# The even chunk's h stays in PSUM, small copies move to ScalarE, and batch 0's routed pairs are done as seven products

## What is computed

```python
def L0(x, y, weight, mask, bias):
    w_bot = einsum('bg,got->bot', y, weight * mask[None])
    return einsum('bnt,bot->bno', x, w_bot) + bias

def L1(x, router_logits, skill_gate, skill_up, skill_down, shared_gate, shared_up, shared_down):
    rw = softmax(router_logits); w, sel = top_k(rw, 2); w = w / w.sum(-1)
    dense_w = zeros((B, E)).at[arange(B)[:, None], sel].add(w)
    mlp = lambda x, g, u, d: einsum('bsi,ih->bsh', gelu(einsum('bsh,hi->bsi', x, g)) * einsum('bsh,hi->bsi', x, u), d)
    out = sum over e of dense_w[:, e] * mlp(x, skill_gate[e], skill_up[e], skill_down[e])
    return out + mlp(x, shared_gate, shared_up, shared_down)

x = x + L0(x, cond_8, weight, mask, bias)
x = x + L1(x, cond_8, skill_..., shared_...)
```

## Time and profile before

| | |
|---|---|
| median of 3 runs | 427.54 us (426.96 to 427.88) |
| the profiled execution | 427.97 us, its span 426.0 us |
| granted clock of PE | 0.999 over the span |
| PE busy | 414.5 us |
| DVE busy | 318.6 us |
| POOL busy | 273.3 us |
| ACT busy | 223.9 us |
| DMA | 36.24 MB, mean 85 GB/s |

### The profile page before, as it was taken

The page is one execution under the profiler, slowest core; times in us unless marked ns, Lnnn a source line. Parts: engine busy times, 40 slices in busy tenths (PEclk is TensorE's granted clock), DMA queues, the critical chain, the costliest instruction groups (busy, mean ns, idle before and its releaser), DMA issues.

```text
span 426.0 us, 6965 instructions
## 1 busy us (share of the span) xinstructions
PE 414.5 (97%) x2133; PEld 349.1 (82%) x2133; DVE 318.6 (75%) x459; ACT 223.9 (53%) x407; POOL 273.3 (64%) x271
## 2 busy tenths in 40 slices
PE   8999999999999999999999899999999999999997
PEld 6688888888888887788888688788888788888886
DVE  3566543334369998887888999988787888888885
ACT  5665555444434366654554347646555445557441
POOL 1565364487603579999626748999771866998820
PEclk9999999999999999999999999999999999999999
DMA  7763243234201513223100252222200041232001
GB/s 254 225 191 138 58 125 99 74 101 123 75 0 51 174 40 118 91 75 102 25 26 0 76 170 74 74 74 83 89 25 25 0 149 49 76 106 69 25 26 49
DMA packets 20187, 36.24 MB, mean 85 GB/s; under 512 B 2242, under 2 KB 3010, under 8 KB 20162
## 3 DMA queue, kind: packets, MB, share of 16 engines
q1 hardware_dynamic: 19872, 35.66, 27.3%
q10 hardware_dynamic: 290, 0.26, 0.2%
HBM read 33.82 MB, written 2.10 MB: 84 GB/s over the span
## 4 chain that ended last, share of the span: by engine, by line
PE 66%; DVE 18%; issue 9%; ACT 4%; DMA 1%; SPq 1%; DVEq 0%; ACTq 0%
PE o_ps L556 7%; PE g_ps L503 7%; PE g_ps L502 7%; PE g_ps L506 7%; PE u_ps L506 7%; PE u_ps L502 7%; PE u_ps L503 7%; PE o_ps L563 7%; PE p_ps L563 5%; DVE h_lo L1027 4%; ACT h_hi L764 3%; DVE h_lo L1037 2%; PE l_ps L461 2%; DVE l_ps L955 2%; DMA l_raw<-l_w 1%
## 5 line engine op out<-in xcount | busy, mean ns | idle before, releaser
L1200 POOL TENSOR_TENSOR eg_lo<-raw_g,eg_hi 128x512 fp32r<-128x512 f32 x64 | 89.2, 1408 | 43.9 <-ACT eg_hi L711 43.9
L740 ACT ACTIVATE gelu<-g_ps 128x512 f32<-128x512 f32 x96 | 57.4, 598 | 47.2 <-PE g_ps L506 46.8
L759 ACT CAST h_hi<-u_ps 128x512 fp32r<-128x512 f32 x34 | 20.0, 588 | 79.2 <-DVE u_ps L986 44.9
L986 DVE SCALAR_TENSOR_TENSOR u_ps<-gelu,route_cur,u_ps 128x512 f32<-128x512 f32 x42 | 31.5, 749 | 34.6 <-PE u_ps L506 32.8
L1037 DVE TENSOR_TENSOR h_lo<-t_raw,h_hi 128x1024 fp32r<-128x1024 f32 x34 | 51.8, 1525 | 6.5 <-ACT h_hi L764 6.4
L764 ACT CAST h_hi<-t_raw 128x1024 fp32r<-128x1024 f32 x34 | 35.7, 1051 | 32.8 <-DVE t_raw L1023 32.8
L1239 POOL TENSOR_TENSOR ed_lo<-raw_d,ed_hi 128x384 fp32r<-128x384 f32 x22 | 36.8, 1671 | 22.1 <-ACT ed_hi L720 22.1
L503 PE MATMUL g_ps<-x_hi,eg_lo 128*128 128x512 f32 (+1 forms) x128 | 50.4, 394 | 0.0
L502 PE MATMUL g_ps<-x_hi,eg_hi 128*128 128x512 f32 (+1 forms) x128 | 50.1, 391 | 0.0
L502 PE MATMUL u_ps<-x_hi,eg_hi 128*128 128x512 f32 (+1 forms) x128 | 49.8, 389 | 0.0
L503 PE MATMUL u_ps<-x_hi,eg_lo 128*128 128x512 f32 (+1 forms) x128 | 49.8, 389 | 0.0
(11 more groups left out here) (234 smaller groups left out, 1130.0 us busy)
## 6 DMA issues: line engine op xcount, KB each, us to landing
raw_g<-experts SPq DMA_DIRECT2D x64, 256.0 KB, 2.7
raw_d<-experts SPq DMA_DIRECT2D x32, 256.0 KB, 2.8
l_raw<-l_w SPq DMA_DIRECT2D x8, 256.0 KB, 5.7
x_in<-xT SPq DMA_DIRECT2D x8, 256.0 KB, 4.3
raw_g<-shared SPq DMA_DIRECT2D x8, 256.0 KB, 4.4
raw_d<-shared SPq DMA_DIRECT2D x8, 256.0 KB, 2.9
outT<-out_sb SPq DMA_DIRECT2D x6, 256.0 KB, 3.0
mask<-l_mask SPq DMA_DIRECT2D x2, 128.5 KB, 6.2
```

What stands on the lines that cost most here:

```text
L740: act.activation(gelu[:, s % 2], g_ps[:], ACT.Gelu_apprx_tanh).then_inc(gelu_done, 1)
L1200: pool.tensor_tensor(eg_lo[:, j % RING], raw_g[:, j % RAW_G], eg_hi[:, j % RING].bitcast(F32), ALU.subtract).then_inc(gu_lo_done, 1)
```

## The change

In fast pairs the even chunk's h is formed in place in `u_ps[:, 0]`; `h_a` goes. Its first half is read from PSUM by ACT (high part) and DVE (T1, low part); its second half is copied by ACT into the small SBUF tile `b12`, which T1 and T3 read. PE's wait ahead of the up projection into `u_ps[:, 0]` becomes one for the low part of h. ACT's order in a fast step becomes gelu, split_t, split of h, b12, then the weights; gate and up weights are split two by two in odd steps, on ACT and POOL. `pick_cond` and `pick_route` go from DVE to ACT. In batch 0, pairs 4 to 11 (the routed ones) become fast: POOL gets `expert_s` and the split of the S parts for them, its gate and up splits from step 8 on go two by two into odd steps, and ScalarE, DVE and POOL drain its sums as those of the other batches are. P5 moves from the PSUM bank of P4 to that of P1; P1 and P5 are copied out in one instruction. The sums of a batch on POOL are seven instructions in place of five. In the last batch DVE's adds are arranged anew. Semaphore counts follow.

```diff
         def fast(b, p):
 
-            return not at_first(b) and not (at_last(b) and p >= LAST_FAST)
+            return not (at_first(b) and p < PAIRS) and not (at_last(b) and p >= LAST_FAST)
+
+        def first_fast(b, p):
+            return at_first(b) and p == PAIRS
...
-                if s < 2 and not at_first(b):
-                    was_fast = not (isinstance(b, int) and b == 1)
-                else:
-                    was_fast = fast(b, s // 2 - 1)
-                if was_fast and s % 2 == 0:
-                    pe.wait_ge(h_done, n - 1)
-                elif was_fast:
+                was_fast = not at_first(b) if s < 2 else fast(b, s // 2 - 1)
+                if was_fast and s % 2:
                     pe.wait_ge(t_done, 4 * pair_count(b, s // 2 - 1) + 4)
...
             def products_123(b, p):
                 wait_d(b, p)
                 pe.wait_ge(h_lo_done, STEPS * b + 2 * p + 2)
-                if p == 0:
+                if first_fast(b, p):
                     pe.wait_ge(x1_done, HH)
-                    pe.wait_ge(out_done, 1)
-                    pe.wait_ge(evac_done, 4 * b)
-                first, last = p == 0, p == (LAST_FAST - 1 if at_last(b) else NP - 1)
+                elif p == 0:
+                    pe.wait_ge(evac_done, 3 * b - 1)
+                last = p == (LAST_FAST - 1 if at_last(b) else NP - 1)
                 wt = d_weights(p)
-                product(P1, wt, None, A11, B11, first, last)
-                product(P2, wt, None, A12, B21, first, False)
-                product(P3, wt, None, S4, B22, False, last).then_inc(down_done, 1)
+                product(P1, wt, A11, B11, p == 0 or first_fast(b, p), False)
+                product(P2, wt, A12, B21, p == 0, False)
+                product(P3, wt, S4, B22, False, last).then_inc(down_done, 1)
 
             def products_4567(b, p):
                 pe.wait_ge(t_lo_done, pair_count(b, p) + 1)
                 if p == 0:
-                    pe.wait_ge(out_done, HH)
-                    pe.wait_ge(evac_done, 4 * b + 2)
-                    if not (isinstance(b, int) and b == 1):
-                        pe.wait_ge(x1_p4_done, b - 1)
-                first, last = p == 0, p == (LAST_FAST - 1 if at_last(b) else NP - 1)
+                    pe.wait_ge(evac_done, 3 * b)
+                    pe.wait_ge(x1_p4_done, b)
+                last = p == (LAST_FAST - 1 if at_last(b) else NP - 1)
                 wt = d_weights(p)
-                product(P6, wt, None, S2, T2, first, False)
-                product(P7, wt, None, S3, T3, False, last)
-                product(P4, wt, None, A22, T4, first, False)
-                product(P5, wt, None, S1, T1, False, last).then_inc(down_done, 1)
+                product(P5, wt, S1, T1, False, last)
+                product(P6, wt, S2, T2, p == 0 or first_fast(b, p), False)
+                product(P7, wt, S3, T3, False, last)
+                product(P4, wt, A22, T4, p == 0, last).then_inc(down_done, 1)
...
-                act.copy(h_hi[:, 0:TH], h_a[:, 0:TH]).then_inc(h_hi_done, 1)
+                act.copy(h_hi[:, 0:TH], u_ps[:, 0, 0:TH]).then_inc(h_hi_done, 1)
+                if not first_fast(b, p):
+                    act.wait_ge(t_done, 4 * pair_count(b, p))
+                act.copy(b12[:], u_ps[:, 0, TH:T]).then_inc(b12_done, 1)
...
-            def evacuate_123(b):
+            def evacuate_23(b):
 
                 act.wait_ge(down_done, STEPS * b + STEPS - 1)
-                act.copy(stage_1, P1).then_inc(evac_done, 1)
+                act.wait_ge(d_lo_done, d_index(b + 1, 0))
                 act.copy(stage_23, o_ps[:, 0]).then_inc(evac_done, 1)
 
-            def evacuate_4567(b):
+            def evacuate_1567(b):
                 act.wait_ge(down_done, STEPS * b + STEPS)
+                act.copy(stage_15, p_ps[:, 0]).then_inc(evac_done, 1)
                 act.copy(stage_67, p_ps[:, 1]).then_inc(evac_done, 1)
-                act.copy(stage_5, P5).then_inc(evac_done, 1)
...
-                    if SPLIT_LEAD <= s < SPLIT_LEAD + ECH:
+                    if SPLIT_LEAD <= s < CHUNKS:
+                        split_gu(0, s - SPLIT_LEAD)
+                    if CHUNKS <= s < SPLIT_LEAD + ECH and s % 2:
+                        split_gu(0, s - SPLIT_LEAD - 1)
                         split_gu(0, s - SPLIT_LEAD)
...
-                    if s < 2 + ECH:
+                    if s % 2 and s < 2 + ECH:
+                        split_gu(b, s - 3)
                         split_gu(b, s - 2)
 
+            def pick_cond(b):
+                act.copy(cond_cur[:], cond_all[:].rearrange("p b e -> p (b e)")[:, bass.ds(b * G, G)]).then_inc(cond_picked, 1)
+
+            def pick_route(b):
+                if at_first(b):
+                    act.wait_ge(weighed, 8)
+                else:
+                    act.wait_ge(h_done, STEPS * b)
+                act.copy(route_cur[:], route_w[:, bass.ds(b * TOP_K, TOP_K)]).then_inc(route_picked, 1)
+
...
-                weights_beside(b, s)
                 if not fast(b, s // 2):
+                    weights_beside(b, s)
                     split_h(b, s)
                 elif s % 2 == 0:
                     split_b11(b, s // 2)
+                    weights_beside(b, s)
                 else:
                     split_b2(b, s // 2)
+                    weights_beside(b, s)
+                if s == CHUNKS - 1:
+                    pick_route(b)
                 if with_next:
                     next_beside(b, s)
 
...
             def form_t1(b, p):
-                if not (isinstance(b, int) and b == 1 and p == 0):
+                if not first_fast(b, p):
                     dve.wait_ge(t_lo_done, pair_count(b, p))
-                dve.wait_ge(h_done, STEPS * b + 2 * p + 1)
-                dve.tensor_tensor(t_part(T1), h_a[:, TH:T], h_a[:, 0:TH], ALU.subtract).then_inc(t_done, 1)
+                dve.wait_ge(b12_done, pair_count(b, p) + 1)
+                dve.tensor_tensor(t_part(T1), b12[:], u_ps[:, 0, 0:TH], ALU.subtract).then_inc(t_done, 1)
 
             def form_t234(b, p):
-                dve.tensor_tensor(t_part(T3), u_ps[:, 1, TH:T], h_a[:, TH:T], ALU.subtract).then_inc(t_done, 1)
+                dve.tensor_tensor(t_part(T3), u_ps[:, 1, TH:T], b12[:], ALU.subtract).then_inc(t_done, 1)
                 dve.wait_ge(t_done, 4 * pair_count(b, p) + 1)
...
-                dve.tensor_tensor(h_lo[:, 0:TH], h_a[:, 0:TH], h_hi[:, 0:TH].bitcast(F32), ALU.subtract).then_inc(h_lo_done, 1)
+                dve.tensor_tensor(h_lo[:, 0:TH], u_ps[:, 0, 0:TH], h_hi[:, 0:TH].bitcast(F32), ALU.subtract).then_inc(h_lo_done, 1)
...
-            def store_ready_0(oh):
-                dve.wait_ge(x1_done, HH)
-                if oh == 0:
-                    dve.wait_ge(sum0_done, 1)
-                else:
-                    dve.wait_ge(down_done, STEPS)
-                dve.tensor_tensor(out_sb[:, oh], x1_at(x1, 0, oh), o_ps[:, oh], ALU.add).then_inc(out_done, 1)
...
+                at, n = (b % 2) * (HH * T) + T, T if at_first(b) else TH
+                dve.wait_ge(down_done, STEPS * b + STEPS)
+                dve.tensor_tensor(x1[:, bass.ds(at, n)], x1[:, bass.ds(at, n)], o_ps[:, 1, 0:n], ALU.add).then_inc(x1_p4_done, 1)
...
+            def add_products_23():
 
                 b = B - 1
                 dve.wait_ge(stored, 16 * HH * b + 1)
                 dve.wait_ge(x1_done, HH * B)
                 dve.wait_ge(down_done, STEPS * b + 2 * LAST_FAST - 1)
-                dve.tensor_tensor(out_flat, x1_all(b).rearrange("p (q c) -> p q c", c=TH), P1.unsqueeze(1).to_broadcast([P, 4, TH]), ALU.add).then_inc(rest_done, 1)
-                dve.wait_ge(rest_done, 1)
-                dve.tensor_tensor(out_sb[:, 0], out_sb[:, 0], o_ps[:, 0], ALU.add).then_inc(rest_done, 1)
-
-            def add_products_6():
+                dve.tensor_tensor(out_sb[:, 0], x1_at(x1, b, 0), o_ps[:, 0], ALU.add).then_inc(rest_done, 1)
+
+            def add_products_46():
                 dve.wait_ge(down_done, STEPS * (B - 1) + 2 * LAST_FAST)
+                dve.tensor_tensor(out_sb[:, 1, 0:TH], x1_at(x1, B - 1, 1)[:, 0:TH], P4, ALU.add).then_inc(rest_done, 1)
+                dve.tensor_tensor(out_sb[:, 1, TH:T], x1_at(x1, B - 1, 1)[:, TH:T], P6, ALU.add).then_inc(rest_done, 1)
                 dve.wait_ge(rest_done, 2)
-                dve.tensor_tensor(out_flat[:, 1:4], out_flat[:, 1:4], P6.unsqueeze(1).to_broadcast([P, 3, TH]), ALU.add).then_inc(rest_done, 1)
-
-            def add_products_457():
-                dve.wait_ge(rest_done, 3)
+                dve.tensor_tensor(out_flat[:, 1:3], out_flat[:, 1:3], P6.unsqueeze(1).to_broadcast([P, 2, TH]), ALU.add).then_inc(rest_done, 1)
+
+            def add_products_157():
+                dve.wait_ge(rest_done, 4)
                 dve.tensor_tensor(out_flat[:, 2:4], out_flat[:, 2:4], P7.unsqueeze(1).to_broadcast([P, 2, TH]), ALU.add).then_inc(rest_done, 1)
-                dve.wait_ge(rest_done, 4)
```

(40 more changed lines are left out.)

122 lines of the change are left out of this document (42 added, 80 removed).

## The result

The changed kernel takes 429.63 us (median of 6 runs, 429.5 to 429.98) where the kernel before took 427.62 us beside it (6 runs, 426.96 to 428.27): a ratio of 1.0049, 95% interval 1.0037 to 1.0062. It is slower by 2.0 us; 422.2 was predicted, and the range ended at 427.5. The profiled execution has a span of 427.5 us, 1.5 more than before.

The account below looks back on a forecast made before the run. PE was taken as the bound, busy 414.5 of 426.0 us, losing 11.0 us to late DVE work. Terms -10.3 - 1.3 + 6.3 = -5.3 us off the 427.54 median gave 422.2 us, range 417.5 to 427.5.

Parts of the forecast that it names:

- h in PSUM: T1 and h's low part on DVE take 415 ns each with one PSUM input; 10.3 us gained, ends 7 and 11.
- the 11.0 us: PE's time lost in batches 1 to 3 against undisturbed pairs of 8.00 us: 3.05 + 5.35 + 2.56.
- both covers: T1's wait for b12 hidden behind DVE's 1024-wide split; the even chunk's PSUM bank freed with 1.6 us or more to spare.
- rival (d): Even chunk's bank or b12 not covered, no gain from PSUM in batches 1 to 3: 432.5 us, chance 0.02.
- Weights behind h: ScalarE's new order, two by two: POOL starts later, but the chain closes under 8.0 us per pair; nothing charged.
- rival (c): The DVE, ScalarE, POOL ring becomes the period, 8.5 us in all 30 routed pairs: 15 us more, 437, chance 0.10.
- The ring's sum of 7.55: One odd h to the next through ScalarE and POOL: 0.75 + 0.6 + 0.6 + 2.6 + 1.8 + 1.2 us.
- Batch 0's eight pairs: Routed pairs of batch 0 as seven products: 8 x (8.16 - 8.00) = 1.3 us gained on PE.
- The tail of batch 0: From step 17 POOL also has the shared weights' S parts: cost 5 to 8.5 us, 6.3 taken, lower end 1.9.
- the two loads: Down weights 5 and 6 in batch 0, sent only after POOL's split; 3.2 to 4.5 us counted for weight 5.
- The last batch's adds: DVE has one wide add less before chunk 21's h and one more after; ends about the same: nothing.
- Sums of batch 0 at the turn: POOL does them beside batch 1's first pairs, some 8.5 us in seven instructions; nothing on the path.

Follow-up runs that it names:

- p3_plain_weights_first: Changed kernel without its batch 0 part, with the gate and up weight splits one by one and ScalarE's ahead of h again: 416.8 us, repeat 416.73.
- p4_s_first: Changed kernel with POOL's S sums ahead of its gate and up splits in odd steps of batches 1 to 3: 425.18 us.
- p5_plain_s_first: Changed kernel without its batch 0 part, with POOL's S sums ahead of its gate and up splits in batches 1 to 3: 416.72 us.
- p10_half_routed: p3_plain_weights_first with pairs 4 to 7 of batch 0 as seven products, pairs 8 to 11 plain: 416.28 us, repeat 416.5.
- p7_weights_first: Whole changed kernel, batch 0 included, with ScalarE's weight casts ahead of h, one per step on ScalarE and POOL: 423.64 us.
- p8_narrow_shared_s: Changed kernel with POOL's S sums of the shared down weights over 8 columns instead of 128: 425.61 us.
- p6_d_before_gu: Changed kernel with batch 0's down weights 5 and 6 loaded ahead of the next batch's gate and up chunks 0 and 2: 429.63 us.
- p14_after_add_behind_h: Changed kernel with DVE's last addition of P1 moved behind the forming of chunk 22's h: 429.42 us.
- p13_add_behind_h: p10_half_routed with DVE's last addition of P1 moved behind the forming of chunk 22's h: 415.45 us.
- p9_split_in_two: Changed kernel with DVE's 1024-column subtraction issued as two of 512 columns: 428.69 us.
- p11_order_alone: Kernel before the change with only the gate and up weight splits two by two and behind ScalarE's part of h: 430.75 us.

## Why the prediction was wrong

The sum was -10.3 - 1.3 + 6.3. Point by point:

*h in PSUM.* Right in its rows (416 and 415 ns for 415) and in the path: with the circle cut, batches 1 and 2 take 98.72 or 98.83 and the ten pairs 80.00, that is, all of the 11.0 us come back, with the small copies, which alone had brought 1.2; I had charged 0.7 for L1037. The some 65 ns more for a PSUM source, worked out from the Trainium skill (VectorE: DVE Perf Modes, section on the TRN2 errata), do not show: L1020 takes 416 ns where the old L1027 took 0.43 us undisturbed. T1's wait for b12 took 1.0 us in 42 instructions, and no gap in front of an even chunk's up projection appeared: both covers held, rival (d) is out.

*Weights behind h: the step that failed.* The text said "It closes under 8.0, so I charge nothing", and against rival (c) "the S sums fall beside L1037 and are short". The ring's sum of 7.55 was right for undisturbed instructions: 8.50 measured less the 0.98 that L1184 waits is 7.52. What failed is the single term 1.8 for the S sums, which took 2.8 (392.15 to 394.98). Falling beside L1037 is no reason for being short but the very thing that makes them long; before, the sums ended just as L1037 began (a mean of 487 ns), and against it the new order moved them by 2.0 us, under it. I had carried the lesson of the earlier trace rows to DVE's two short instructions and not to POOL's side of the same contention. Cost: 6.0 gained instead of 10.3, 4.3 us off the forecast and 5.0 off the 11.0 that were there; p3_plain_weights_first, p4_s_first and p5_plain_s_first give back 4.6, 4.5 and 4.7 us. Rival (c) was the right mechanism with the right period (8.5), but not "in all 30 routed pairs": only four pairs of the last batch and two in each of the others show it. So in batches 1 to 3 its price was 5.0, not 15. As I read it, the circle needs the splits of next weights beside the S sums, and no slack left over: in the last batch, where no first layer of a next batch gives PE 1.38 us twice, two pairs more are long. No run isolates this.

*Batch 0's eight pairs.* Priced 1.3 gained; four of them gained 0.82 on PE in p10_half_routed, so this holds. But already before the tail two of the pairs lost 0.36 and 0.50 us (PE again waits for gelu; in p7_weights_first and p10_half_routed both are gone), 0.9 that was not in the sum.

*The tail of batch 0.* 6.3 predicted. By the starts of PE's product groups the profiled execution loses 8.3 there: 6.6 in waits and the restarts behind them, and 1.7 in the matmuls from 112 to 115, which start every 0.43 us instead of 0.23. The reasons were half right. The S sums of the shared weights beside those of the pairs are the cause (p8_narrow_shared_s, p10_half_routed), but the two loads, from which I worked out 7.5 to 9 and 21.4 to 24.4, do not decide (p6_d_before_gu): POOL is busy for 13.6 of 14 us there. (Their sum had a slip as well: 3.2 to 4.5 us after 3.8 are 7.0 to 8.3, and the 0.5 to 0.7 above that stand in no row.) Of the 29.2 us counted for POOL nothing was counted as disturbed; L1199 alone took 1 us more beside DVE's L1030. That the low clock costs its 1.7 us in the end is not shown: the executions of this kernel without the low stretch took as long as those with it. My estimate is that where POOL sets the pace, a slower PE only shortens the wait that follows; there is no trace of an execution without the stretch to show it. So batch 0 stands at 117.45 - 109.77 = 7.7 where 5.0 was predicted, and how the difference divides beyond the 0.9 of the two early pairs stays open.

*The last batch's adds.* "It ends at about the same time ... Nothing" was wrong by 0.4 us, and has its own runs (p14_after_add_behind_h, p13_add_behind_h). I compared when the last addition ends with the final products, and not with the h of chunk 22 that is queued behind it.

*Sums of batch 0 at the turn*: nothing, as predicted (batch 1 takes 98.72 in p4_s_first).

Together: 4.3 for the circle, 7.7 - 5.0 = 2.7 for batch 0 and 0.4 for the adds, less the 0.5 by which PE started earlier, is 6.9 above -5.3, so +1.6 where the spans say +1.5. Of the signs to look for, "pitch 8.00 in batches 1 to 3" failed and "even gaps with gelu late behind a ScalarE split of s_raw (c)" came. The chance of 0.10 for it was too low: the prediction had its ring within 0.45 us of the period, with a term in it that the text itself called disturbed.

## What to carry to other kernels

Where instructions of several in-order engines close a circle once per step, sum it with the durations that its instructions have at their new place, disturbed by what now runs beside them, and not with undisturbed ones; here a slack of 0.45 in 8.00 us, by undisturbed durations, was none. When contention is taken from one engine, look for who on the other engine was waiting in the same way, and which of the two has somebody behind it. And do not put optional work (here four pairs, each worth 0.16 us) into the only stretch where an engine already does one-time work: where POOL had room, four of them gained, and the other four cost some 2 us each.

## What the runs showed of the hardware

DVE's and POOL's instructions that use SBUF alone exclude each other for a whole instruction, not in shares: a 128-column POOL instruction takes 1.44 us when it starts 0.14 us after a 1.27 us DVE instruction, and 0.46 undisturbed; a DVE instruction of 1.22 us takes 2.06 behind a POOL instruction of 1.02. DVE's 256-column L1009 and L1020, which took 933 and 1333 ns on average with both inputs in SBUF, stayed at 0.40 to 0.42 us in all 84 cases with one input in PSUM, beside a busy POOL too. Cut in two (p9_split_in_two), the long instruction lets the other engine in once, and pays for it itself: 0.94 us for its second half, where the first took 0.73. The Trainium skill says the same (SBUF — State Buffer, section "SBUF: two separate sides"): for a VectorE instruction with two SBUF inputs against a GpSimd one that reads SBUF, the one that starts first holds the shared ports for the whole instruction and the other blocks. The rows agree, both ways round: POOL was held up in the changed kernel, DVE in p3_plain_weights_first.

TensorE's granted clock was 1.00 until 111 us in the profiled execution of the changed kernel although PE had stood for 1.24, 1.23 and 2.21 us before that, and 0.50 (1.2 of 2.4 GHz) from 112 to 115, when PE was busy without a break. In p8_narrow_shared_s, with one gap of 2.25 us and the others at 0.25 or less, it did not fall. One such gap does not settle it either way: behind the turn from batch 1 to 2 it fell in p11_order_alone (a gap of 2.11) and not in the profiled execution of the kernel before (2.13). Nor did it set the time of this kernel: its six executions, four with a mean clock of 1.00 and two with 0.996, all lie between 429.50 and 429.98 us.
